# Channel attention moved from single images to batches of four, with the value convolution read from padded images

## The reference

```python
mu, var over (C, H, W) of each image
xn = (x - mu) * rsqrt(var + EPS) * ln_g + ln_b
# _proj: per head (8 heads of 12 channels) a 12x12 pointwise map with bias, then a depthwise 3x3 convolution with bias
Q, K, V = _proj(xn, wq...), _proj(xn, wk...), _proj(xn, wv...)
logits = einsum('bhnc,bhnd->bhcd', K, Q) / alpha[head]      # 12x12 for each head, summed over 256 points
attn = softmax(logits, axis=-1)
out = einsum('bhnc,bhcd->bhnd', V, attn)
return einsum('bcij,oc->boij', out, w_f) + b_f + xn
```

## Time and profile before

| what | us |
|---|---|
| times of three executions | 536.03, 541.72, 536.63 |
| median | 536.63 |
| span of the profiled execution, first to last instruction | 540.4 |
| the execution of the three that lies nearest above that span | 541.72 |
| stage 1, about | 0 to 263 |
| stage 2, about | 263 to 360.4 |
| stage 3, setting up, up to its first convolution | 360.4 to 378.2 |
| stage 3, the images | 378.2 to 540.4 |
| PE busy, share of the span | 96% |

### The profile page before, as it was taken

How to read it: one execution, slowest core, us unless ns; L and a number is a source line. 1 busy time by engine, 2 the same in 40 slices (tenths; PEclk the granted TensorE clock), 3 DMA queues, 4 the chain that set the end, 5 groups by cost and what they waited for, 6 DMA issues and landing times. The chain is left out here.

```text
span 540.4 us, 23612 instructions
## 1 busy us (share of the span) xinstructions
PE 518.1 (96%) x9134; PEld 343.1 (63%) x9134; DVE 365.9 (68%) x1003; ACT 302.1 (56%) x763; POOL 178.3 (33%) x216
## 2 busy tenths in 40 slices
PE   7999999999999999998899999939999999999996
PEld 6777777777777777776674343339655655555553
DVE  1479999999999999997404354436556565656544
ACT  2278877777787778876435563103444444444432
POOL 8433444444434443344200220022433332333300
PEclk8599999999999999999999999957999999999999
DMA  4111111111111101100130132323454434444411
GB/s 83 29 42 32 30 30 46 29 30 30 30 29 24 26 24 29 29 3 2 45 75 21 46 93 71 88 49 79 121 146 124 115 101 118 121 114 105 117 51 32
DMA packets 41177, 32.51 MB, mean 60 GB/s; under 512 B 19240, under 2 KB 36776, under 8 KB 41128
## 3 DMA queue, kind: packets, MB, share of 16 engines
q1 hardware_dynamic: 37544, 26.11, 18.9%
q0 software_dynamic: 3584, 5.72, 4.8%
HBM read 18.36 MB, written 7.13 MB: 47 GB/s over the span
## 5 line engine op out<-in xcount | busy, mean ns | idle before, releaser
L383 POOL TENSOR_TENSOR scores<-scores,peak 128x768 f32<-128x768 f32 x64 | 94.3, 1473 | 135.3 <-DVE peak L552 135.3
L1224 POOL DMA_DIRECT2D x_stack<-padded_x x96 | 52.4, 548 | 97.4 <-PE ps_v L1497 63.4
L446 ACT COPY probs_t<-ps_probs 128x768 f32<-128x768 f32 x64 | 51.1, 799 | 40.7 <-PE ps_probs L706 40.7
L544 DVE TENSOR_TENSOR scores<-ps_scores,bias 128x768 f32<-128x768 f32 x64 | 61.3, 957 | 9.1 <-PE ps_scores L696 7.4
L552 DVE TENSOR_REDUCE peak<-scores 128x12 f32<-128x768 f32 x64 | 61.0, 953 | 2.4
L719 PE MATMUL ps_out<-v_blocks,probs_t 128*64 128x54 f32 x1536 | 57.2, 224 | 1.0 <-ACT out_t L451 0.9
L719 PEld LDWEIGHTS ps_out<-v_blocks,probs_t 128*64 128x64 f32 x1536 | 50.2, 138 | 12.3 <-issue 12.2
L706 PE MATMUL ps_probs<-ident,scores 128*128 128x128 f32 x384 | 55.0, 279 | 0.0
L440 ACT ACTIVATE scores<-scores 128x768 f32<-128x768 f32 x64 | 54.2, 846 | 0.6 <-POOL scores L383 0.6
L1037 ACT ACTIVATE hidden<-ps_hidden,fc_b_folded 128x512 f32<-128x512 f32 x48 | 29.1, 688 | 36.8 <-PE ps_hidden L978 36.8
L1497 PE MATMUL ps_qk<-x_stack,conv_w 40*32 40x256 f32 x1536 | 48.8, 379 | 0.0
(11 more groups left out here) (156 smaller groups left out, 900.2 us busy)
## 6 DMA issues: line engine op xcount, KB each, us to landing
x_stack<-padded_x SPq DMA_DIRECT2D x96, 54.0 KB
x_stack<-padded_x POOLq DMA_DIRECT2D x96, 54.0 KB, 2.7
padded_x<-x_pad SPq DMA_DIRECT2D x32, 121.5 KB, 2.5
x_sliced<-stream SPq DMA_DIRECT2D x48, 64.0 KB, 2.0
mixed<-y_sliced SPq DMA_DIRECT2D x48, 64.0 KB, 2.0
out<-y_sb SPq DMA_DIRECT2D x32, 96.0 KB, 2.0
x_now<-in_x SPq DMA_DIRECT2D x32, 72.0 KB, 1.8
stream<-in_x SPq DMA_DIRECT2D x32, 72.0 KB, 1.9
```

The lines of the kernel that those rows point to most:

```text
L383: nc.gpsimd.tensor_tensor(sc, sc, peak[:, par, p, :].unsqueeze(2).to_broadcast((128, HEADS, WN)), ALU.subtract).then_inc(s["shifted"], 1)
L446: nc.scalar.copy(probs_t[:, :], ps_turned).then_inc(s["turned_copied"], 1)
L544: nc.vector.tensor_tensor(scores[:, par, p, :].rearrange("p (g c) -> p g c", g=NG), ps_scores[:, :, 0:GROUP * WN], bias[:, p, :].rearrange ...
L1224: engine.dma_start(x_stack[64 * half + i * HC:64 * half + (i + 1) * HC, slot, :, :], rows).then_inc(landed[slot], 16)
```

## The change

In stage 3 the channels move to a layout of four pairs of heads: pair p (24 channels) sits on partitions 32p to 32p + 23 of `mixed`, `stats`, `ln_g`, `ln_b`, `x_pad`, `av_sb` and `y_sb`, which become 128 partitions high; the unused rows are zero, but for a row of ones behind each pair of `x_pad` (from `ln_b`), which carries the bias. The images go in batches of four, all written out (no loop).

- v is no longer convolved from `x_stack` but from `x_pad` itself: for each of nine taps 16 matmuls in tiles of 32 x 32, row group = pair, column group = image, 256 points each, into four banks. The nine taps of a batch are dealt out between the batch's other work (1, 2, 2, 1, 2, 1).
- q and k are convolved as before, with heads gathered in pairs.
- `gram` is done once a batch: 4 pairs by 2 halves of the points by 4 images, 32 matmuls with 24 columns in, 24 out; the logits of the wrong head of a pair are masked by `pair_mask`, and one softmax (one add, two reductions, a subtraction, an exponential, a reciprocal, a product) serves four images.
- `attend` is 16 matmuls in tiles of 32 x 32 for a batch, into the banks of v. `finalise` is still one matmul an image, two batches later.
- The tokens are copied by two DVE copies of 192 elements an image. The output is stored by four DMAs a batch.
- In stage 2, `join_y` has to cut each slice of 32 channels at the borders of the pairs: 24 + 8, 16 + 16 or 8 + 24 rows, so each join is two DMAs. POOL clears `mixed` group by group before it.
- The averaging matrix is built by POOL at the start of stage 3 (128 x 128), and PE waits for it; the fills use it. Weight loads grow from 44 to 67.

The core of the diff:

```diff
+PAIR_ROWS = 32
+PAIR_C = 2 * HC
+HEAD_PAIRS = NH2 // 2
+BATCH = 4
+BATCHES = B // BATCH
...
+def join_pieces(c):
+    pieces, at = [], 0
+    while at < 32:
+        pair, inside = divmod(32 * c + at, PAIR_C)
+        rows = min(32 - at, PAIR_C - inside)
+        pieces.append((at, PAIR_ROWS * pair + inside, rows))
+        at += rows
+    return pieces
...
-    LATE = 44
+    LATE = 67
...
-        sp.wait_ge(zeroed_final, 1)
+        sp.wait_ge(zeroed_final, 5)
...
+    JOINED = 2 * PARTS
...
+            sp.wait_ge(mixed_zeroed, g + 1)
             sp.wait_ge(s["mixed_ready"], (g * SLICES + c + 1) * 2)
             for r in range(QUARTERS):
                 at = (g * QUARTERS + r) * CHUNK
-                sp.dma_start(mixed[32 * c:32 * c + 32, at:at + CHUNK],
-                             y_sliced[32 * r:32 * r + 32, g % 2, c, :]).then_inc(y_out[g % 2], 16)
+                for here, there, rows in join_pieces(c):
+                    sp.dma_start(mixed[there:there + rows, at:at + CHUNK],
+                                 y_sliced[32 * r + here:32 * r + here + rows, g % 2, c, :]).then_inc(y_out[g % 2], 16)
...
+        def clear_mixed(g):
+            at = g * QUARTERS * CHUNK
+            nc.gpsimd.memset(mixed[:, at:at + QUARTERS * CHUNK], 0.0).then_inc(mixed_zeroed, 1)
+        clear_mixed(0)
         for g in range(1, GROUPS):
             for r in range(QUARTERS):
                 scale_tokens(nc, pool, m, s, g, r)
+            clear_mixed(g)
...
-SLOTS = 4
-AHEAD = 6
...
+AHEAD = 5
...
+    average = sb("average3", [128, 128])
...
-    ps_v_banks = bank("ps_v3", ROUNDS)
...
+    ps_v_banks = bank("ps_v3", HEAD_PAIRS)
...
+    ps_tok = ps_qk_banks[:, :, N:2 * N]
...
+        def store(b, par):
+            sp.wait_ge(s["y_ready"], (b + 1) * BATCH)
+            for p in range(HEAD_PAIRS):
+                sp.dma_start(out[bass.ds(b * BATCH, BATCH), p * PAIR_C:(p + 1) * PAIR_C].rearrange("t c h w -> c t (h w)"),
+                             y_sb[pair_rows(p), par, :, :]).then_inc(out_done[par], 16)
...
+        nc.gpsimd.memset(average[:, :], 0.0).then_inc(zeroed, 1)
+        pool.wait_ge(zeroed, 1)
+        for p in range(HEAD_PAIRS):
+            nc.gpsimd.memset(average[pair_rows(p), :], 1.0 / C).then_inc(averaged, 1)
+        pool.wait_ge(averaged, HEAD_PAIRS)
         nc.gpsimd.memset(eps[:, :], EPS).then_inc(zeroed, 1)
...
+        def copy_v(b, par):
+            act.wait_ge(s["v_ready"], b + 1)
+            need(act, s["av_ready"], b - 1)
             nc.scalar.copy(v_sb[:, par, :, :], ps_v).then_inc(s["v_copied"], 1)
...
+        def copy_av(b, par):
+            act.wait_ge(s["av_ready"], b + 1)
+            need(act, s["final_ready"], (b - 1) * BATCH)
+            nc.scalar.copy(av_sb[:, par, :, :], ps_v).then_inc(s["av_copied"], 1)
...
+        def step(b, par):
+            for i in range(BATCH):
+                if i == 3:
+                    copy_v(b, par)
+                copy_qk(b * BATCH + i)
+                if i == 0 and not is_image(b, 0):
+                    exponent(b - 1)
+                if i == 2 and not (isinstance(b, int) and b + 2 >= BATCHES):
+                    take_moment(b + 2, par)
+                if i == 3 and not is_image(b, 0):
+                    copy_av(b - 1, 1 - par)
+                t, later, slot, side = ahead(b, i, par)
+                if not past(t):
+                    pad_x(t, later, slot, side)
...
+            turned = ps_tok.rearrange("p n (e q c) -> p n e q c", e=2, c=32)
+            for kind in range(2):
+                nc.vector.tensor_copy(tokens[:, i, :, kind, :, :, :].rearrange("p n q e c -> p n e q c"),
+                                      turned[:, :, :, :, kind * HC:(kind + 1) * HC]).then_inc(s["tok_copied"], 1)
...
+        def shift_logits(b):
+            dve.wait_ge(s["gram_ready"], b + 1)
+            need(dve, s["attn_ready"], b)
+            nc.vector.tensor_tensor(logits[:, :, :], ps_gram, w["pair_mask"][:, :].unsqueeze(1).to_broadcast((128, HEAD_PAIRS, PAIR_C)),
+                                    ALU.add).then_inc(s["masked"], 1)
...
+        def step(b, par):
+            for i in range(BATCH):
+                t, later, slot, side = ahead(b, i, par)
+                if not past(t):
+                    take_gain(t, later, slot, side)
+                    take_offset(t, slot, side)
+                if i == 0 and not is_image(b, 0):
+                    shift_logits(b - 1)
+                copy_tokens(b * BATCH + i, i)
+                if i == 0 and not is_image(b, 0):
+                    normalise(b - 1)
+                if not isinstance(b, int) or b > 1:
+                    finish(b - 2, i, par, ps_y)
...
-        free = ps_av[0:C, 0:C]
+        free = ps_v_banks[:, 3, 0:128]
+        pe.wait_ge(averaged, HEAD_PAIRS)
...
+        def convolve_v(b, par, first, last):
+            if first == 0:
+                pe.wait_ge(s["x_padded"], (b + 1) * BATCH)
+                need(pe, s["av_copied"], b - 1)
+                need(pe, s["v_copied"], b)
+            for tap in range(first, last):
+                down, right = tap // SIDE, tap % SIDE
+                for i in range(BATCH):
+                    for p in range(HEAD_PAIRS):
+                        rows = slice(PAIR_ROWS * p, PAIR_ROWS * (p + 1))
+                        mm = nc.tensor.matmul(ps_v[PAIR_ROWS * i:PAIR_ROWS * (i + 1), p, :], conv_v[rows, tap, :],
+                                              x_pad[rows, par, i, down:down + H, right:right + W],
+                                              start=(tap == 0), stop=(tap == TAPS - 1))
+            if last == TAPS:
+                mm.then_inc(s["v_ready"], 1)
...
+            for p in range(HEAD_PAIRS):
                 for n in range(2):
-                    for k in range(TILE_HEADS):
-                        mm = nc.tensor.matmul(ps_gram[32 * k:32 * k + 32, r, :], tokens[:, n, r, 32 * k:32 * k + 32],
-                                              tokens[:, n, r, 32 * k + HC:32 * k + 2 * HC], start=(n == 0), stop=(n == 1))
+                    for i in range(BATCH):
+                        k, q = (tokens[:, i, n, kind, p, :, :].rearrange("p e c -> p (e c)") for kind in range(2))
+                        mm = nc.tensor.matmul(ps_gram[PAIR_ROWS * i:PAIR_ROWS * i + PAIR_C, p, :], k, q,
+                                              start=(n == 0), stop=(n == 1))
...
+        def attend(b, par):
+            pe.wait_ge(s["attn_ready"], b + 1)
+            pe.wait_ge(s["v_copied"], up_to_batch(b + 1))
+            for p in range(HEAD_PAIRS):
+                for i in range(BATCH):
+                    rows = slice(PAIR_ROWS * i, PAIR_ROWS * (i + 1))
+                    mm = nc.tensor.matmul(ps_v[PAIR_ROWS * p:PAIR_ROWS * (p + 1), i, :], attn[rows, p, :], v_sb[rows, par, p, :],
+                                          start=True, stop=True)
...
+        def step(b, par):
+            first = is_image(b, 0)
+            third = not isinstance(b, int) or b > 1
+            convolve_qk(b * BATCH, b, 0)
+            if not first:
+                gram(b - 1)
+            convolve_v(b, par, 0, 1)
+            turn_tokens(b * BATCH)
+            convolve_v(b, par, 1, 3)
+            if third:
+                finalise(b - 2, 0, par, ps_y)
+            convolve_qk(b * BATCH + 1, b, 1)
+            convolve_v(b, par, 3, 5)
+            turn_tokens(b * BATCH + 1)
+            convolve_v(b, par, 5, 6)
+            if third:
+                finalise(b - 2, 1, par, ps_y)
+            convolve_qk(b * BATCH + 2, b, 2)
+            convolve_v(b, par, 6, 8)
+            turn_tokens(b * BATCH + 2)
+            convolve_v(b, par, 8, 9)
+            if third:
+                finalise(b - 2, 2, par, ps_y)
+            convolve_qk(b * BATCH + 3, b, 3)
+            if third:
+                finalise(b - 2, 3, par, ps_y)
+            if not first:
+                attend(b - 1, 1 - par)
+            turn_tokens(b * BATCH + 3)
+        batch_loop(pe, step)
+        finalise(BATCHES - 2, 0, 0, ps_y)
+        gram(BATCHES - 1)
+        for i in range(1, BATCH):
+            finalise_last(BATCHES - 2, i, 0, late_homes[i])
+        attend(BATCHES - 1, 1)
+        for i in range(BATCH):
+            finalise_last(BATCHES - 1, i, 1, last_homes[i])
```

482 lines of the change are left out of this document (237 added, 245 removed).

## The result

The changed kernel takes 575.15 us (median of 4 runs, 570.49 to 579.36), against 539.17 (536.03 to 542.93, 4 runs) for the kernel before in the same comparison: a ratio of 1.069, 95% interval 1.059 to 1.080. The prediction was 537 with a range of 523 to 553: wrong, 38 us too low and outside the range. Executions of one kernel differ by some 7 us with TensorE's granted clock in stage 1 (0 to 280 us), which is 0.96 in both profiled executions here and 0.96 to 1.00 in those of the experiments.

The account below looks back on a forecast made before the run. PE was taken to bound stage 3, SP's queue the end of stage 2. 541.7 - 18.8 + 14.8 + 4.6 = 542.3 us profiled; the change alone, +0.6 on 536.6, gave 537, range 523 to 553.

Parts of the forecast that it names:

- Part 2: End of stage 2: each join becomes two DMAs, 96 issues for 48 on SP's queue; loss 14.8 us.
- Part 3: Start of stage 3: wait for the averaging matrix, larger fills and more small records on PE; loss 4.6 us.
- the twenty records: PE's fills at the start of stage 3, at half clock: 4.3 us for 3.45.
- the 56: 56 records on PE at the start of stage 3: 6.15 us for 4.92.
- The forty records: PE's fills at the start of stage 3: 7.0 us instead of 6.6, 26 at half, the rest at full clock.
- Part 1: Stage 3: PE takes 17.0 us for a batch of four images against 19.6; gain 18.8 us.
- All sixteen run together, a tap is two rounds: v convolution in stage 3: a tap's 16 matmuls overlap, each round 0.216 us; nine taps in six chunks 5.15 us.
- the rival of tiles that don't fill the array: Stage 3: only eight tiles at once, 571 us; milder, second eight trail by a round, 546; chance 0.23.
- Only batch 0 has bare places: Stage 3: copies are covered by PE work except 0.3 and 0.95 us in batch 0 and 0.3 in batch 1.
- the third rival, PE waits in stage 3: Stage 3: copies, a gather or the unrolled program's supply hold PE up 1 us a batch; +8, 545 us; chance 0.15.
- Cheap joins: End of stage 2: join pieces cost SP only 0.35 to 0.45 us, loss 1 to 6, 524 to 529 us; chance 0.20.

Follow-up runs that it names:

- The last run: Complete kernel with joins from both queues, tokens ahead of attend, nine single v chunks; fills cut, one more quarter of the third group's joins on GpSimd: 547.47 us, ratio 1.022.

## Why the prediction was wrong

**Part 2, the joins: mechanism right, size off.** Predicted loss 14.8, measured 23.6. The mis-sized term is the price of a piece, "I take 0.59". That was the duration of a whole join, while the chain needs the time from start to start, for which the same sentence had read 0.633. The pieces follow one another at 16.73 / 24 = 0.70 (group 1) and 34.44 / 48 = 0.72 (the end): above the upper bound of 0.633. The bound was drawn from whole joins, as if a piece could cost at most what the whole does. For 16 rows that holds (0.59, start to start 0.63), for 8 rows nearly (0.625, 0.67), for 24 rows not (0.73, 0.77). Why 24 rows cost more than 32 is open. At 72 us of loss for each us of price, which the prediction's own two figures give (17.9 at 0.633, 14.8 at 0.59), 0.70 to 0.72 make 22.7 to 24.2. The chain behind it (moments ahead of residuals in VectorE's program, the last pieces behind both) held.

**Part 3, the start of stage 3: the sum right, in part by luck.** Predicted 4.6, range 3.6 to 5.5, measured 4.0. The wait for the averaging matrix (+1.2), the twenty records (+1.2) and the 56 (+1.5) came somewhat dearer than put. Two terms were further off and against each other. The forty records were to take 7.0 for 6.6 and took 4.65 for 6.44 from start to next start. The clock was to rise 10.5 us after PE had begun ("I keep that"), and rose at 390.9, 6.9 us behind the stage's first issue and 5.6 behind PE's first matmul. The turning of the weights up to the 56 was to take 0.3 less and took 3.99 for 2.52, 1.5 more, with the 72 small records alone at 2.1 (predicted 0.8). The last run shows besides that shorter fills take 4.7 us off this start.

**Part 1, stage 3: wrong in sign.** Predicted a gain of 18.8, measured a loss of 9.6, 28.4 between them:

- *"All sixteen run together, a tap is two rounds" held for a single tap* (0.65 predicted and measured, gram, attend, finalise, tokens and q/k within 0.03), so the rival of tiles that don't fill the array fell in its hard form. *It failed for a second tap*: 0.78 instead of 0.43, 24 chunks of two at 0.35 each, 8.4 us. With half the columns a second tap still takes 0.56, where its two rounds would be 0.22, so it isn't the streaming alone. A tap is 64 instructions; that those of the first stand ready while the block before it works would explain the difference, but no run shows it by itself.
- *"Only batch 0 has bare places"* failed. I checked the cover of ScalarE's copy before each token turn, and of VectorE's copy as "a finalise and one tap or more over them". Behind the fourth image stands neither: its turn is the last step, and the next batch's q and k need its bank. That is a wait of 0.81, and a block of 1.46 in place of 0.58, 0.88 in each of seven batches: 6.2 us. The new order of the tokens took the wait down to 0.16.
- *The supply of the unrolled program* was named in the third rival with one word and priced with the copies at 8 us for all. The sum of what the v chunks take over the undisturbed 0.65 and 1.43 is 11.1 us over eight batches; 1.1 of it are the single taps of batches 0 and 1, which have no finalise behind them, and the other 10.0 are the breaks. That late instructions make them is shown by the loop over single batches, where no fetch and no break is left.
- The tail took 13.2 for 12, and 1.5 us are spread over the rest. 8.4 + 6.2 + 11.1 + 1.2 + 1.5 = 28.4.

Of the rivals, "PE waits in stage 3" came nearest: +8 was its price, +17 (6.2 and 11.1) is what those waits cost. "Cheap joins" was on the wrong side. The sum joined three wrong terms that all pointed the same way, and the range of 523 to 553 was made from them one at a time.

On the Trainium skill's queue of 64 entries (TensorE: Matmul & The Clock Gate, Part 2), which would "just hold 16 float32 matmuls": the rows agree with it, at 0.65 for the first tap and 0.78 for the second, though no run tests it apart from other causes. I used the rule for the first tap and did not carry it to the second.

**Settled:** the joins, the cover of the tokens, the late instructions. **Open:** why the second tap costs 0.78 and the third 0.63 when the half columns cost 0.56, which is 8.4 us of the 28.4; and why instructions come late: by how much other transfers delay a fetch (without gathers 2.3 us of stage 3 went, in one profile, and the last batch, with hardly a transfer, has no break). That the added empty instructions took no room left the direct test, more instructions for the same work, undone.
